# A wait in front of each group of row gathers in a four-layer graph network

## The reference

```
x = LN(x + L0(x))  # Q,K,V; score = <Q[dst],K[src]>/4 for 8 heads; softmax over dst; sum of alpha*V[src]; FFN
x = LN(x + L1(x))  # two layers: segment_sum(x[src]*w, dst) + x, divided by the count; two matmuls; leaky ReLU
x = LN(x + L2(x))  # three GATv2 layers (4, 4, 1 heads), below
x = LN(x + L3(x))  # segment_sum(x[src]*norm*w, dst), matmul, GELU, LN
# one GATv2 layer:
xl = x @ Wl + bl
e  = leaky_relu(xl[src] + (x @ Wr + br)[dst]);  logits = sum(e * att) per head
a  = softmax of logits over the edges of one dst
h  = segment_sum(xl[src] * a, dst) + c
```

## Time and profile before

| what | value |
|---|---|
| median, lowest, highest of three runs | 6167.75, 6162.48, 6183.69 us |
| the profiled execution, first to last instruction (its span) | 8199.2 us |
| score loop in it | 203 to 1923 us |
| fused passes in it | 2936 to 4512, 4637 to 6231, 6349 to 7902 us |
| mean granted TensorE clock | 0.656 of full |

### The profile page before, as it was taken

How to read it: one execution, slowest core, us unless ns; L and a number is a source line. 1 busy time by engine, 2 the same in 40 slices (tenths; PEclk the granted TensorE clock), 3 DMA queues, 4 the chain that set the end, 5 groups by cost and what they waited for, 6 DMA issues and landing times. The chain is left out here.

```text
span 8199.2 us, 128493 instructions
## 1 busy us (share of the span) xinstructions
PE 5007.5 (61%) x25366; PEld 3730.4 (45%) x25375; DVE 4287.8 (52%) x10883; ACT 2730.0 (33%) x6600; POOL 3533.6 (43%) x3882
## 2 busy tenths in 40 slices
PE   2677777774888935555556345555555355655557
PEld 2555555553664524444444334444444244444443
DVE  6555555556664145555555545554556445555554
ACT  1333333333542003333334323333334133333342
POOL 2544444442320044555554445555552555555520
PEclk7676677776999965555556556555556555555568
DMA  2444444443444722222222122222221222222215
GB/s 72 128 137 135 137 134 139 134 137 86 134 134 158 249 54 58 64 62 62 65 59 61 42 54 63 62 59 66 60 63 35 54 60 61 60 60 61 58 35 202
DMA packets 579250, 728.81 MB, mean 89 GB/s; under 512 B 90091, under 2 KB 424769, under 8 KB 578686
## 3 DMA queue, kind: packets, MB, share of 16 engines
q0 software_dynamic: 123968, 282.81, 14.9%
q1 hardware_dynamic: 304800, 350.53, 14.5%
q10 hardware_dynamic: 149918, 88.82, 4.0%
HBM read 601.07 MB, written 120.75 MB: 88 GB/s over the span
## 5 line engine op out<-in xcount | busy, mean ns | idle before, releaser
L1769 POOL DMA_INDIRECT rows<-scratch_gat,index x2496 | 2437.4, 977 | 2757.1 <-DVE mix L1997 1461.9
L2103 PE MATMUL sums<-xr_part,hot_t 128*128 x7524 | 1106.9, 283 | 786.2 <-issue 466.9
L2158 PE MATMUL sums<-mix,vhot 128*128 128x128 f32 x4992 | 1261.8, 421 | 91.0 <-issue 81.7
L2103 PEld LDWEIGHTS sums<-xr_part,hot_t 128*128 128x128 bf16 x7524 | 775.5, 121 | 1102.7 <-issue 945.7
L2011 DVE TENSOR_TENSOR z<-sums,rows 128x512 f32<-128x512 f32 x624 | 428.7, 687 | 1563.0 <-remote 1425.4
L1836 ACT ACTIVATE moved_sums<-sums x624 | 373.1, 598 | 2620.8 <-remote 1599.0
L932 POOL DMA_INDIRECT rows<-scratch_kv,index_ring x832 | 820.6, 986 | 887.5 <-ACT index_ring L1242 661.3
L2158 PEld LDWEIGHTS sums<-mix,vhot 128*128 128x128 f32 x4992 | 1044.4, 303 | 186.6 <-issue 142.6
L1368 PE MATMUL sums<-at_hot,lo_hot 128*128 128x200 f32 x2496 | 820.1, 493 | 16.4 <-issue 11.2
L1826 ACT ACTIVATE vhot<-iota,edge_local 128x128 f32<-128x128 f32 x2496 | 791.2, 392 | 0.1
L2154 PE MATMUL sums<-zeros 128*128 128x8 bf16 x624 | 114.7, 184 | 999.9 <-issue 551.5
(11 more groups left out here) (514 smaller groups left out, 6385.9 us busy)
## 6 DMA issues: line engine op xcount, KB each, us to landing
piece<-scratch_adj SPq DMA_DIRECT2D x90, 1280.0 KB, 6.3
local_ring<-scratch_local_rows SPq DMA_DIRECT2D x633, 128.0 KB
scratch_spool<-rows ACTq DMA_DIRECT2D x208, 256.0 KB, 2.6
vals<-scratch_spool SPq DMA_DIRECT2D x208, 256.0 KB, 2.6
scratch_adj<-stage SPq DMA_DIRECT2D x25, 1600.0 KB
rows<-scratch_gat,index POOLq DMA_INDIRECT x2496
local_ring<-scratch_local_rows ACTq DMA_DIRECT2D x211, 128.0 KB
mask<-scratch_masks SPq DMA_DIRECT2D x234, 80.1 KB
```

Of the source, the lines that this page charges most:

```text
L1769: eng.indirect_dma_start(rows[:, slot, q, k * LINE:(k + 1) * LINE], None, table, bass.IndirectOffsetOnAxis(ap=index[:, slot, s:s + 1], axis=0)
L2103: ins = eng.matmul(B.ps[:, at + k * D:at + (k + 1) * D], hot_t[:, slot, k * P:(k + 1) * P], part[:, bass.ds(at_block, D)], start=(j == 0), ...
L2158: ins = eng.matmul(B.ps[:, bass.ds(of_block * D, D)], hot[:, v % MIXES, k * P:(k + 1) * P], mix[:, v % MIXES, k * D:(k + 1) * D], start=Fa ...
```

## The change

In the fused passes GpSimd waits, ahead of the gathers of each group, until the gathers of the group before have landed (the group before the first of a portion is the last of the portion before; the very first group of a pass has none). In the score loop it does so for every second group, the odd ones; the even ones stay as they were. On ScalarE one field of a table is now taken out with two register instructions into a register of its own instead of an expression; nothing else differs.

```diff
@@ score loop, GpSimd @@
                         for q in range(2 * h, 2 * h + 2):
                             eng.wait_ge(kept[q].sem, kept[q].at(0) + i * 16)
+                            if q % 2:
+                                for s in range((q - 1) * GROUP, q * GROUP):
+                                    eng.wait_ge(landed[s].sem, landed[s].at(16) + i * 16)
                             eng.sem_inc(wait_holder.sem, 1)
                             for s in range(q * GROUP, (q + 1) * GROUP):
                                 gather_rows(B, eng, rows, table, width, s, landed)
@@ score loop, ScalarE @@
+                need = eng.alloc_register(f"need{B.fresh()}")
...
-                            need = field(twos[0], NEED_FIELD.bit_length() - 1, 32, BLOCKS - 1)
-                            eng.wait_ge(room.sem, need + (room.at(0) + 1))
+                            eng.reg_alu(need, twos[0] // NEED_FIELD, 31, ALU.bitwise_and)
+                            eng.wait_ge(room.sem, eng.snap(need, min_val=0, max_val=BLOCKS - 1) + (room.at(0) + 1))
...
-                for r in sum(regs, []):
+                for r in sum(regs, []) + [need]:
                     eng.free_register(r)
@@ fused pass, GpSimd @@
                         eng.wait_ge(mixed.sem, mixed.at(1 + q) + p * PORTION_GROUPS)
+                        if q:
+                            before, turns = landed[slot * PORTION_GROUPS + q - 1], turn
+                        else:
+                            before, turns = landed[(slot - 1) % RING_PORTIONS * PORTION_GROUPS + PORTION_GROUPS - 1], turn - (slot == 0)
+                        if q or not (isinstance(p, int) and p == 0):
+                            eng.wait_ge(before.sem, before.at(16 * GROUP) + turns * (16 * GROUP))
                         eng.sem_inc(wait_holder.sem, 1)
                         for k in range(GROUP):
                             s = q * GROUP + k
```

## The result

The changed kernel takes 7832.94 us (7827.49 to 7836.06, four runs), the kernel before beside it 6175.36 us (6162.48 to 6183.69, four runs): ratio 1.270, 95% interval [1.2675, 1.2716]. The forecast was 7544 us in a range of 6600 to 7850.

What follows compares the result with a forecast made beforehand. GpSimd's queue of gathers was taken to bound the fused passes in a timed run. The base of 6168 us plus 1329 for the fused passes and 47 for the score loop gave 7544 us, range 6600 to 7850.

Steps and rivals of the forecast that it cites:

- GpSimd's queue bounds the fused passes in a timed run: Fused passes before the change: GpSimd's four gathers, 5.15 us a group, set the timed pace, taken as 5.2.
- A group costs 7.33 us with the wait: Fused passes after the change: gathers 4.84, landing 1.7 and restart 0.79 us, between 5.63 and 7.63.
- Tail: Fused group: landing of the last gather after GpSimd is through with it, 1.7 us, between 0 and 2.0.
- tail and restart together: GpSimd's gap before each waiting group: landing 1.7 plus 0.79 us to start again, about 2.5 us.
- The fused term: Three fused passes: 2.13 us more for each of 624 groups, +1329 us.
- The score loop costs 47 us: Score loop: GpSimd's pair of 13.05 us against consumers' 12.6, +0.45 x 104 = 47 us, range 0 to 150.
- The gap in the middle of a pair: Score loop: GpSimd's wait before the odd group, landing 1.7 plus restart 0.79, about 2.5 us.
- the restart of 0.81 us at the next pair's indices: Score loop: GpSimd's start after ScalarE has written indices, 0.81 us of the 13.05 us pair.
- TensorE's stalls are absent from timed runs: Whole kernel: most TensorE issue stalls belong to the profiled execution, since the timed median is 2031 us less.
- The span hardly moves, 8199 to 8350 us: Profiled execution: consumers' 7.57 us against 7.33 a group, so the span goes from 8199 to some 8350 us.
- The rival "hidden": Fused passes: the wait is covered or passes at once, so the time stays at 6170 us; chance 0.09.
- The rival "faster": Fewer gathers under way free TensorE's issue in fused passes and score loop: about 6085 us; chance 0.04.

Runs made afterwards that it cites:

- e10: Kernel before plus the ScalarE edit and, in the fused passes' odd groups alone, a wait behind the first gather: 6538.21 us beside 6153.39, ratio 1.0616.
- e9: Changed kernel with waits moved behind the first gather, in every fused group and the score loop's odd groups: 7092.93 us beside the kernel before's 6153.39, ratio 1.1526.
- e1: Kernel before with the ScalarE register edit alone, no wait added: 8021.09 us beside 8023.35, ratio 0.9999.
- e5: Changed kernel unaltered, timed again beside the kernel before: 7858.44 us beside 8038.96, ratio 0.9774.
- e2: Kernel before plus the ScalarE edit and the new waits in the fused passes alone: 8076.65 us beside 8023.35, ratio 1.0062.
- e7: Kernel before plus the ScalarE edit and, ahead of each fused group, a GpSimd memset pause without a landing wait: 7706.26 us beside 8038.96, ratio 0.9581.
- e4: Kernel before plus the ScalarE edit and, in the fused passes only, the wait behind each group's first gather: 7422.39 us beside 8023.35, ratio 0.9262.

## Why the prediction was right

The number came out with luck in it, in two places. The result's comparison fell on the lower level; beside the upper one the same change is 2.3% faster. And 7832.94 us lies 17 us under the upper end of the range.

*GpSimd's queue bounds the fused passes in a timed run: right for the comparison of the result.* From e10 the kernel before, at its lower level, spends 1216 us in the score loop, from its first to its last use of rows, and 1802 us outside the loops; of 6153 us 3135 are left for the three passes, 5.05 us for each of their 621 intervals from use to use. VectorE's first use of a pass comes 34 us after the first gather and its last one 8 us after the start of the last group of gathers (both in the changed kernel), so GpSimd's own intervals are 26 / 207 = 0.12 us longer, 5.17. GpSimd's four gathers were put at 5.15, and I took 5.2; in the first 24 groups of a pass, where nothing holds it, the kernel before takes 5.21 to 5.23. That agrees, and so do e9 and e10: 6.40 us with a wait in every group and 5.68 in every second one leave 4.97 with none. All this is worked out, not seen in a profile of the kernel before at its lower level.

*A group costs 7.33 us with the wait: right, a little low.* Measured from one L2021 to the next: 7.41 us, from gather to gather 7.54. Tail 1.64 (1.7), tail and restart together 2.35 us in the timeline (2.49); over all groups GpSimd's idle time there is 2.4 us at the median and 2.7 in the mean. The fused term is then 621 x (7.41 - 5.05) = 1466 us, predicted 1329.

*The score loop costs 47 us: mis-sized.* It is 1426 us now against 1216, +210, outside the 0 to 150 that I kept. (That upper end was also added up wrongly: with a tail of 2.0 a pair takes 13.35 us, against 11.6 this is 1.75 x 104 = 182 us, not 146.) Three terms were off. The pace before is 5.87 us a group, not 6.3. I had set it from above TensorE's 6.01, read at a granted clock of 0.71; at e10's 0.85 TensorE is busy for 989 us instead of 1249, and a matmul of the adjacency takes 415 ns instead of 495. The gap in the middle of a pair is 364.9 / 104 = 3.5 us, not 2.5, since these gathers land later. And the restart of 0.81 us at the next pair's indices isn't paid: GpSimd idles 0.30 there. From the view of L932 in the changed kernel:

```profile
DMA to landing us min/median/max: 2.6/3.3/7.0
```

Why they land later isn't shown: the rows are longer (1024 bytes against 528) and the DMA engines are busier (0.58 against 0.26), and in e10, with no wait in this loop, the median is 4.0 us.

The sum of the measured terms is 1466 + 210 = 1676 us; the change of the median is 1658. This sum is no test, since the 5.05 is what was left of the kernel before; the test is that 5.05 fits GpSimd's queue. The forecast was short by 289 us: 137 in the fused term and 163 in the score loop's, less some 11, mostly because the base was 6168 and not 6153.

*TensorE's stalls are absent from timed runs: right by all signs where the result was measured, wrong as a reason.* They have nothing to do with the profile being taken, as e1 shows. The time of 6168 us told that those runs hadn't got them, and that was all it told.

*The span hardly moves, 8199 to 8350 us: wrong.* It fell from 8199.2 to 7829.6. I had argued 7.57 against 7.33 us a group, and no gain in the score loop. The fused passes did about stay (4629 to 4603 us between uses of rows, summed), and the score loop gave 286 of the 370 us, since its stalls went with the waits (354 late loads before, none now). These two profiles stand at different levels; at the upper one, from e1 to e5, the span falls by 171 us: 223 less in the score loop, 71 more in the passes, 19 less outside.

*The rival "hidden", given 0.09.* At the upper level that is nearly what the waits in the passes are: e2 costs 53 us. They don't pass at once, since VectorE idles 1921 us there for rows; they cost about what the stalls did.

*The rival "faster", given 0.04.* Its mechanism exists: gathers issued without a pause stall TensorE, and the change removes this. It is what the change does at the upper level (0.9774). Its price was bounded by the wrong step: I let the timed pace be at most 5.69 us, so that the new pace of 7.33 could never win. At the upper level the old pace is 7.21 us in the passes, where the change about breaks even (7.33 in e5), and 8.17 in the score loop, where it wins (7.09 in e5). I had asked for a tail of nothing, and the tail is 1.64 us.

What stays open: what decides the level. All runs of the kernel before in one comparison have the same, one chip has shown both, and nothing tried here shows what sets it. Nor is it shown why TensorE's instructions come late while GpSimd issues. That the stalls are tied to runs of gathers is shown: at the upper level the passes have 526 late loads in e1, 295 in e7, 72 in e4 and none in e2. The path between them isn't.

## What to carry to other kernels

A queue that is busy for 43% of a profile can be the bound: add its busy time and its unavoidable gaps for one group, and set that beside the pace of the timed run, not of the span. A wait for a landing ahead of a running queue of gathers costs the tail and the restart, 2.35 us here per group, and its lead over the consumer is lost; behind the first gather it costs rather more than half of that (1.35 us a group in e9 against 2.36), and for two groups back next to nothing, as measured at the upper level alone. If span and timed median differ by a third, the kernel may have two levels: time it more than once beside each version before a verdict is trusted.

## What the runs showed of the hardware

While GpSimd issues indirect gathers back to back, TensorE can fall to single weight loads 0.7 to 1.4 us apart, in e1 from 5 us after the run begins at the earliest to 2.3 us behind its end at the latest. At the start of a pass, where GpSimd fills the whole ring, this lasts longest: the first eight groups take 109 us in e1, 34 in e2, 25 in e4. Whether it happens differs between comparisons of one and the same program: 8023 us against 6153. With nothing to wait for, GpSimd starts a gather every 1.26 us (0.96 busy, 0.30 between), and a gather of 528-byte rows lands 2.6 us after its issue at the median.
